# A fused recommendation tower: units of work reordered in phases, preparation on a second DMA queue, gathers paced by products instead of memsets

## What is computed

```python
e = jnp.stack([tbl_f[ids[:, f]] for f in range(39)], axis=1)      # 2048 x 39 x 32
p, q = e[:, ROW, :], e[:, COL, :]                                # the 741 pairs i < j
z = jnp.einsum('bpc,apc,bpa->bp', p, w, q)                       # w: 32 x 741 x 32
h = jnp.concatenate([z, dense_ctx], axis=1)                      # 741 + 16
h = jnp.maximum(h @ W_top1 + b_top1, 0.0)                        # 757 -> 512
h = jnp.maximum(h @ W_top2 + b_top2, 0.0)                        # 512 -> 256
y = h @ W_top3
```

## Time and profile before

| | |
|---|---|
| median of three runs | 873.27 us |
| profiled execution, and its span | 877.21 us, 875.4 us |
| TensorE busy | 734.8 us (84%) |
| VectorE busy | 655.0 us (75%) |
| ScalarE busy | 92.4 us (11%) |
| GpSimd busy: gathers, memsets | 382.3 us, 207.6 us |
| DMA | 149.90 MB, mean 171 GB/s |
| mean granted TensorE clock | 0.93 of 2.4 GHz |

### The profile page before, as it was taken

How to read it: one execution, slowest core, us unless ns; L and a number is a source line. 1 busy time by engine, 2 the same in 40 slices (tenths; PEclk the granted TensorE clock), 3 DMA queues, 4 the chain that set the end, 5 groups by cost and what they waited for, 6 DMA issues and landing times.

```text
span 875.4 us, 11491 instructions
## 1 busy us (share of the span) xinstructions
PE 734.8 (84%) x4378; PEld 291.6 (33%) x4378; DVE 655.0 (75%) x786; ACT 92.4 (11%) x153; POOL 589.1 (67%) x752
## 2 busy tenths in 40 slices
PE   2603567387998969999999699999999799999998
PEld 1201122122332424443433244444433244444333
DVE  4603759466989947899898679999999478998750
ACT  2202000110010101010101111001111010111002
POOL 6899999998169999997599999982999940000000
PEclk9856688788999989999999899999999899999999
DMA  6677663658654567633664647444734575326000
GB/s 162 207 267 271 216 199 106 224 169 288 229 171 159 157 198 227 228 123 101 228 185 154 199 145 244 136 143 164 248 107 154 189 240 172 142 70 207 22 0 1
DMA packets 71036, 149.90 MB, mean 171 GB/s; under 512 B 12782, under 2 KB 22081, under 8 KB 70853
## 3 DMA queue, kind: packets, MB, share of 16 engines
q1 hardware_dynamic: 58684, 142.83, 47.0%
q0 software_dynamic: 12288, 6.32, 5.0%
q10 hardware_dynamic: 8, 0.01, 0.0%
HBM read 115.49 MB, written 33.62 MB: 170 GB/s over the span
## 4 chain that ended last, share of the span: by engine, by line
PE 64%; DMA 14%; DVE 12%; issue 5%; SPq 4%; ACT 1%; DVEq 0%; ACTq 0%
PE z_ps L541 21%; PE u_ps L517 20%; PE t_ps L495 8%; PE m_ps L554 7%; DVE prod L773 6%; DVE one_hot L761 5%; DMA e<-scratch 5%; DMA w_rows<-h 3%; DMA scratch<-parts 3%; PE m_ps L556 2%; DMA hot_idx<-hot 2%; PE t_ps L480 1%; SPq L412 1%; PE u_ps L576 1%; PE u_ps L585 1%
## 5 line engine op out<-in xcount | busy, mean ns | idle before, releaser
L773 DVE TENSOR_TENSOR prod<-u_ps,eT 128x1024 f32<-128x1024 f32 x400 | 469.7, 1216 | 127.6 <-PE u_ps L517 126.6
L330 POOL DMA_INDIRECT e_rows<-in_tbl_dram,idx x384 | 382.3, 996 | 121.4 <-issue 65.3
L517 PE MATMUL u_ps<-e,w 128*128 128x512 f32 x800 | 263.0, 443 | 97.0 <-DMA e<-scratch 50.6
L541 PE MATMUL z_ps<-prod,sel 128*32 128x512 f32 x1600 | 268.7, 624 | 0.0
L517 PEld LDWEIGHTS u_ps<-e,w 128*128 128x128 f32 x800 | 135.6, 195 | 244.2 <-issue 114.4
L337 POOL MEMSET pause<- 128x512 f32 x364 | 207.6, 570 | 0.2
L495 PE MATMUL t_ps<-one_hot,tb 125*32 125x512 bf16 x1560 | 150.2, 399 | 28.2 <-DVE one_hot L761 27.8
L761 DVE TENSOR_SCALAR one_hot<-hot_idx,row 125x512 bf16<-125x512 f16 (+2 forms) x320 | 155.2, 539 | 20.0 <-DMA hot_idx<-hot 16.1
L495 PEld LDWEIGHTS t_ps<-one_hot,tb 125*32 125x32 bf16 x1560 | 56.3, 101 | 124.4 <-issue 82.6
L541 PEld LDWEIGHTS z_ps<-prod,sel 128*32 128x32 f32 x1600 | 44.5, 110 | 141.4 <-issue 122.6
L554 PE MATMUL m_ps<-zT,w1s 128*128 128x512 f32 x144 | 73.2, 592 | 0.0
(11 more groups left out here) (42 smaller groups left out, 101.9 us busy)
## 6 DMA issues: line engine op xcount, KB each, us to landing
w<-w_rows SPq DMA_DIRECT2D x100, 512.0 KB, 5.4
e<-scratch SPq DMA_DIRECT2D x72, 512.0 KB, 4.9
scratch<-parts SPq DMA_DIRECT2D x72, 256.0 KB, 2.2
w_rows<-h SPq DMA_DIRECT2D x24, 512.0 KB, 6.3
e_rows<-in_tbl_dram,idx POOLq DMA_INDIRECT x384
hot_idx<-hot SPq DMA_DIRECT2D x12, 512.0 KB, 6.8
h<-in_w_dram SPq DMA_DIRECT2D x6, 512.0 KB, 4.5
e<-scratch SPq DMA_DIRECT2D x8, 384.0 KB, 4.1
```

Source lines behind the costliest of these rows:

```text
L330: pool.indirect_dma_start(e_rows[:, r, n, D * q:D * q + D], None, tables[f], bass.IndirectOffsetOnAxis(ap=idx[:, t, f * TPG + n:f * TPG + ...
L517: last = nc.tensor.matmul(u_ps[:, s % 2, place, :], w4[:, p % WR, (u % PW) * P:(u % PW + 1) * P], e4[:, chunk_no(t, g) % ES, j - C * g, :] ...
L541: last = nc.tensor.matmul(z_ps[D * quad:D * quad + D, z % 2, :], sel[:, D - 1 - row:2 * D - 1 - row], prod[:, (NS * t + n) % PR, place, :] ...
L773: nc.vector.tensor_tensor(prod[:, s % PR, :, :], u_ps[:, s % 2, :, :], e, ALU.mult).then_inc(s_mul, 1)
```

## The change

**Order of units.** UNITS is built by PHASES = (0, 1, 2, 3, 7, 8, 4, 5, 6, 9): a phase takes the fields of its chunk against all chunks seen so far, and the fields of earlier, higher-numbered chunks against its own. So the looked-up chunks 7 and 8 come before the gathered chunks 4, 5 and 6. Chunks 3, 7, 8, 4, 5, 6 and 9 are first needed as `e4` in batches 5, 9, 13, 21, 28, 36 and 42; chunks 4, 5 and 6 are needed as `eT` two batches before that. The look-ups in FIRST_TILE and OTHER_TILES move with them, mostly two slices per batch, and the pieces of the dense network fill the other batches.

**Slots.** `e4` has four slots, given by chunk (E4_SLOT), so that chunks 0, 1 and 2 of the next tile find theirs free before the tile ends; only chunk 3 waits for chunk 9. The ring of weight pieces shrinks from six to four.

**Preparation.** The weights come in 13 preps of 16 units, in two rooms used in turn. Their DMAs, and those of the tables, are issued by ScalarE. The network's weights are loaded at batch 12 of tile 0.

**Gathers.** Memsets follow gathers only while fewer than 96 were issued. From the 97th gather on (number n counted from 0), GpSimd waits until product n - 39 is done.

```diff
-ES = 3
+ES = 4
+PACED_FROM, PACE_LEAD = 96, 40
+E4_SLOT = {0: 0, 1: 2, 2: 3, 3: 1, 7: 2, 8: 3, 4: 0, 5: 1, 6: 0, 9: 1}
-PREPS = {0: (2,), 3: (3,), 11: (4,), 19: (5,), 27: (6,)}
-PREP_UNITS = [(0, 8)] + [(8 + 32 * k, 40 + 32 * k) for k in range(6)]
+PREP_UNITS = [(16 * k, min(NU, 16 * k + 16)) for k in range(-(-NU // 16))]
+PREPS_FIRST = 3
+PREPS = {4 * (k - PREPS_FIRST): k for k in range(PREPS_FIRST, len(PREP_UNITS))}
-OTHER_TILES = ((3, 0, 0, ()), (4, 0, 3, ()), (5, 0, 7, ()), (6, 0, 12, ()),
-               (7, 0, None, (13, 14, 15, 16, 17, 18, 19, 19, 20, 20)), (8, 0, None, (21, 22, 23, 24, 25, 26, 27, 27, 28, 28)),
+OTHER_TILES = ((3, 0, 0, ()), (7, 0, None, (1, 1, 2, 2, 3, 3, 4, 4, 5, 5)), (8, 0, None, (6, 6, 7, 7, 8, 8, 9, 9, 10, 10)),
+               (4, 0, 14, ()), (5, 0, 20, ()), (6, 0, 27, ()), (9, 0, 35, ()),
...
                     for n in range(TPG):
+                        if issued >= PACED_FROM:
+                            pool.wait_ge(s_mul, issued - PACE_LEAD + 1)
                         pool.indirect_dma_start(
...
-                        if GPOS[c] > 1:
+                        issued += 1
+                        if GPOS[c] > 1 and issued < PACED_FROM:
                             if paused:
                                 pool.wait_ge(s_pause, paused)
                             nc.gpsimd.memset(pause[:, :], 0.0).then_inc(s_pause, 1)
...
+            def weights_rest(k):
+                a, b = PREP_UNITS[k]
+                act.wait_ge(s_wlo, k + 1)
+                for h in range(2):
+                    act.dma_start(w_rows[:, h, 1, a * P:b * P].rearrange("a (s n) -> a s n", s=C),
+                                  w_in_room[k % 2][:, 0:(b - a) * D]).then_inc(s_wout[k % 2], 16)
+                if k + 2 < len(PREP_UNITS):
+                    load_weights(k + 2)
...
+            def load_weights(k):
+                a, b = PREP_UNITS[k]
+                if k >= 2:
+                    act.wait_ge(s_wout[k % 2], 64 * (k // 2))
```

More of the change, by code:

```diff
@@ L23, in fields_in, with hot, gathered @@
     return min(C, F - C * g)
[L27 to L32, removed]
+HOT_TABLES = {1: ((0, 8), (1, 10), (2, 8), (3, 8)), 2: ((1, 8), (2, 8), (3, 8)), 7: ((0, 10), (1, 8), (2, 8), (3, 8)),
+              8: ((0, 10), (1, 8), (2, 10), (3, 10))}
+HOT_CHUNKS = sorted(HOT_TABLES)
+HOT_SLICES = {g: tuple(n for q, n in HOT_TABLES[g]) for g in HOT_CHUNKS}
+def hot(c):
+    return c[1] in HOT_TABLES
+def gathered(c):
+    taken = [q for q, n in HOT_TABLES[c[1]]] if hot(c) else []
+    return [q for q in range(fields_in(c[1])) if q not in taken]
 def slices_of(g):
-    return max(HOT_SLICES[g][1])
+    return max(HOT_SLICES[g])
 def slice_fields(g, k):
-    return [x for x, n in enumerate(HOT_SLICES[g][1]) if n > k]
+    return [x for x, n in enumerate(HOT_SLICES[g]) if n > k]
 HOT_COLS = {}
@@ L132, in rows_count, with e4_before, e4_loads @@
     n = GPOS[c]
-    return sum(16 * TPG * gathered(GATHERED[x][1]) for x in range(n % ER, n + 1, ER))
+    return sum(16 * TPG * len(gathered(GATHERED[x])) for x in range(n % ER, n + 1, ER))
+def e4_before(c):
+    t, g = c
+    same = [x for x in PHASES if E4_SLOT[x] == E4_SLOT[g]]
+    n = same.index(g)
+    return (t, same[n - 1]) if n else (t - 1, same[-1]) if t else None
+def e4_loads(c):
+    same = [x for x in PHASES if E4_SLOT[x] == E4_SLOT[c[1]]]
+    return len(same) * c[0] + same.index(c[1]) + 1
 TURNS, TAKES, COMPLETE, INDICES, STACKS = {}, {}, {}, {}, {}
@@ L166, in spread_mlp @@
         slices = sum(list(x[3]).count(b) for x in OTHER_TILES if not (last and x[1]))
-        work[b] = 3 * slices + (2 if any(x[2] == b for x in OTHER_TILES) else 0)
+        work[b] = 3 * slices + (3 if any(x[2] == b for x in OTHER_TILES) else 0)
     taken = []
@@ L238, in tower @@
         hroom = h1[:, :, :].rearrange("p m n -> p (m n)")
-        w_in_room = hroom[:, 0:2 * NB]
-        w_hi_room = hroom[:, 2 * NB:4 * NB].bitcast(F32R)
+        w_in_room = [hroom[:, k * NB:(k + 1) * NB] for k in range(2)]
+        w_hi_room = [hroom[:, (2 + k) * NB:(3 + k) * NB].bitcast(F32R) for k in range(2)]
         ids_f = prod[:, 0, :, :].rearrange("p u n -> p (u n)")[:, 0:NT * HOT_FIELD_COLS]
         def table_room(g):
-            first, rows = HOT_ROWS[g, 0], sum(HOT_SLICES[g][1])
+            first, rows = HOT_ROWS[g, 0], sum(HOT_SLICES[g])
             if g == HOT_CHUNKS[-1]:
@@ L321, in _ @@
             paused = 0
+            issued = 0
             for c in GATHERED:
@@ L477, in turn @@
                     pe.wait_ge(s_et, POS[c])
-                n = D * gathered(c[1])
+                lo, hi = D * gathered(c)[0], D * (gathered(c)[-1] + 1)
                 for b in range(TPG):
-                    last = nc.tensor.transpose(t_ps[0:n, b * P:b * P + P], e_rows[:, GPOS[c] % ER, b, 0:n], ident[:, :])
+                    rows = e_rows[:, GPOS[c] % ER, b, lo:hi]
+                    if lo == 0:
+                        last = nc.tensor.transpose(t_ps[0:hi, b * P:b * P + P], rows, ident[:, :])
+                    else:
+                        last = nc.tensor.matmul(t_ps[lo:hi, b * P:b * P + P], rows, ident[:, :], start=True, stop=True,
+                                                skip_group_check=True)
                 last.then_inc(s_tp, 1)
@@ L486, in look_up @@
                     pe.wait_ge(s_et, POS[c])
-                if k == 0 and t == 0:
+                if k == 0:
                     pe.wait_ge(s_tlo, HOT_CHUNKS.index(g) + 1)
@@ L595, in _ @@
             transpose_ids()
-            for g, turned, slices in BEGIN:
-                if turned:
+            for g in BEGIN:
+                if gathered((0, g)):
                     turn((0, g))
-                for k in slices:
-                    look_up((0, g), k)
+                if hot((0, g)):
+                    for k in range(slices_of(g)):
+                        look_up((0, g), k)
             pe.wait_ge(s_sel, 16)
```

221 lines of the change are left out of this document (111 added, 110 removed), and 2 rows, old and new, of the table OTHER_TILES.

## The result

The changed kernel takes 842.04 us (841.25 to 842.87, four runs), the kernel before 874.83 in the runs beside it: a ratio of 0.963, with a 95% interval of 0.9605 to 0.965. The forecast was 808, with a range of 784 to 842. The sign was right, but the gain is 33 us and not 67, and the time lies at the range's far end. The profiled execution has a span of 839.4 us, against 875.4.

The account below looks back on a forecast made before the run. No engine full: tile 0 bound by a chain of waits in SyncE's queue, later tiles near TensorE's work, VectorE in some batches. Stalls and clock -27.9, late chunks +4.5, look-ups +5.5, opening and tile 0 -49.3: -67.2, giving 808, range 784 to 842.

Parts of the forecast that it names:

- the walk: Step-by-step timing of opening and tile 0 through the programs; with 6 us added for queueing, tile 1 starts at 251.
- Part 1, the stalls: Batch 2 of tiles 1 to 3: four slots remove waits for chunk 2, 21.9 us, or 27.9 with the clock.
- The slow clock behind the stalls: Tiles 1 to 3: one group of sums takes 3.25 us where 1.07 is usual; 2 each, 6 in all.
- Part 1, late chunks: Tiles 1 to 3: chunk 8, at times 7, a little late; 1.5 us per tile, +4.5, bounds 0 and 5 per tile.
- Part 2 and 3, pairs and memsets: Tiles 1 to 3: paired look-ups lengthen VectorE-bound batches, missing memsets cheapen one-hots; together +1.2, +1.2, +3.1, or +5.5.
- rival B: One-hots: gathers alone hold them up as gathers with memsets did; time 825, chance 0.10.
- Part 4: Opening and tile 0: shorten from 300.3 to 251 us, gain 49.3; ends 232 and 275.
- prep 2's stores land at 58: Opening: stores take 5 us to land (bounds 3.2 and 10.3), at 58; first products at 60 us.
- a count of megabytes up to batch 14: Opening and tile 0: some 30 MB, 120 us at 249 GB/s, under 138, so DMA bandwidth isn't the bound, though near.
- A: Tile 0: ScalarE becomes the gate, nine preps cost 3 us more each; time 835, chance 0.17.
- C: Turns behind tile 0: paced gathers come late, slower than before; 892 at 4 late, 934 at 6; chance 0.05.
- D: Opening and tile 0: the timing is too careful, tile 0 ends at 232; time 789, chance 0.10.

Follow-up runs that it names:

- experiment 8: Kernel before with only the look-ups of the next tile's chunks 1 and 2 moved earlier, chunk 2's done in batch 47 instead of 49: 851.92 us, ratio 0.974.
- (9): Kernel before with both four slots given by chunk and the earlier look-ups of experiment 8: 849.72 us, ratio 0.972.
- (7): Kernel before with four slots given by chunk and four rooms for weight pieces, look-ups and memsets as before: 871.68 us, ratio 0.996.
- Experiment 2: Changed kernel with the look-ups of chunk 8 in tiles 1 to 3 dealt one batch earlier: 830.8 us, ratio 0.951 to the kernel before.
- (3): Changed kernel with the edits of gate and Experiment 2 together: 819.72 us, ratio 0.940 to the kernel before.
- three_first: Kernel of (3) with chunk 3 turned in batch 0 of tile 0, ahead of chunk 7's look-ups: 807.93 us, ratio 0.925 to the kernel before.
- (4): Changed kernel with memsets between the gathers kept throughout and no pacing by products: 871.2 us, ratio 0.998 to the kernel before.
- gate: Changed kernel with ScalarE issuing raw weights of preps 4 and 5 after tile 0's casts, not behind landings of preps 2 and 3: 829.93 us, ratio 0.950.
- Experiment 12: The run of three_first: kernel of (3) with chunk 3 turned in batch 0 of tile 0, ahead of chunk 7's look-ups: 807.93 us, ratio 0.925.
- (5): Changed kernel without the wait that paces gathers by products, still no memsets from the 96th gather on: 840.35 us, ratio 0.962 to the kernel before.
- early_nomem: Kernel of (9) with no memsets from the 96th gather on: 842.41 us, ratio 0.964 to the kernel before.

## Why the prediction was half right

Two terms of the sum failed. Opening and tile 0 were to give 49.3 us and gave 26.4: the walk had the stores of prep 2 landing at 58, and they landed at 73, with ScalarE and behind it the first products waiting. Late chunks were charged 4.5 us in tiles 1 to 3 and cost 9 to 12.

**Part 1, the stalls: near in size, wrong in cause.** They are gone. The forecast was 27.9 us; the table alone gives 22.6 (experiment 8) and with the slots 24.8 (9). But the prediction says that the slot "frees only when the tile before ends", and that four slots take this away. Four slots alone do not (7). The stack stood behind look-ups that ended in batch 49. That the change also ended them in batch 47 I had counted only under the pairs. I read the last condition off the program and did not look which of the two came last; the queue's rows would have told. The slow clock behind the stalls was priced at 2 us each, by a group of sums of another batch (1.07). The same group takes 1.91 without a stall (8), against 3.25, 2.90 and 2.83 with one, so the price is 3.3 us in all and not 6.

**Part 1, late chunks: a term that was mis-sized.** I charged 1.5 us per tile for chunk 8, with 5 as the bound if two chunks were late. The pause is 2.2 to 2.5 us, and the four pieces behind it take 1.3 to 1.5 more. Experiment 2 gives 11 us back (9 in the profiled executions), and with the opening mended too (3) the three tiles are 3.4, 3.3 and 4.9 us shorter, 11.7 in all. I had priced the slow clock behind the old stalls and not behind the new one.

**Part 2 and 3, pairs and memsets: right for the changed kernel, with the memsets priced too low.** Before, without stall and slow clock (by the 1.91), tiles 1, 2 and 3 take 176.5, 175.9 and 197.5 us. In `three_first`, where chunk 8 is in time, they take 176.8, 176.7 and 200.2: +0.3, +0.8 and +2.7, where the sum said +1.2, +1.2 and +3.1. The one-hot at 351 ns makes rival B wrong. What I had as the price of the memsets, 6.3 us a tile (7.5 less 1.2), is too low: putting them back costs 12.0, 9.1 and 8.9 (4). Beside memsets the wide forms in pairs take 806 ns and not 694, which is a part of it; the rest I can't name.

**Part 4: the steps of the walk.** The walk's marks beside the traces (us; "batch 5" is where it goes on behind its wait):

| | walk | changed | `gate` | `three_first` |
|---|---|---|---|---|
| first product | 60 | 75.1 | 63.5 | 63.2 |
| products of batch 1 | 73 | 87.3 | 76.3 | 76.7 |
| turn of chunk 3 | 81 | 100.2 | 87.6 | 66.0 |
| batch 5 | 99 | 119.5 | 107.6 | 93.8 |
| batch 9 | 120 | 138.2 | 127.2 | 116.0 |
| batch 14 | 138 | 162.6 | 151.7 | 140.4 |
| tile 1 | 251 | 273.9 | 263.2 | 252.2 |

Look-ups began at 20.3 us (forecast 19.4), table 7 was split at 32.0 (31). The step that failed is "prep 2's stores land at 58": 15 us. Chunk 2 was taken at 55.14 and not 49, and one issue took 4.24 us and not 0.6, so the last store went out at 61.37 and not 53, and it landed after 11.76 us and not 5. Around it the DMA engines moved 323 GB/s (55 to 75 us), more than the 249 that I read over a longer stretch. The sum there, a count of megabytes up to batch 14, hid that peak, though the trace of before has one like it:

```profile
75.00:95.00 20.00, 8.24 (x28) 2.94 (x28) 6.09 (x7) 2.12 (x3) 18.01 (x26) 0.67 0.84 304
```

That the traffic made the landing long is argued from the two standing side by side. What is shown is that ScalarE's wait for it costs 12 us (1).

Batch 5 came 20.5 us late: 15 from the start, 4 more in the batches before the turn of chunk 3, and only 1.3 on chunk 3's own way back, 19.3 us from turn to resumption where the walk has 18. The second step that failed is chunk 8 in tile 0: from batch 9 to batch 14 the walk has 18 us and the trace 24.3, with a wait of 6.4 us for chunk 8. No run took that wait away.

Experiment 12 must not be read as mending the walk. The wait on chunk 3 was in the forecast (products of batch 4 at 87, batch 5 at 99); turning chunk 3 first removes a stall that the walk had counted in. With only the failed step mended, in `gate`, tile 1 starts at 263.2. That `three_first` has it at 252.2, beside my 251, is a coincidence of one saving that I had not planned and the losses that remained.

**Rivals.** A named the right engine and the wrong place: ScalarE's waits for landings cost in the opening, not in batches 14 to 36, where VectorE waits 1.3 us in all for the rounding between 162 and 230 us. C did not come: no turn waits on `e_rows`, and the pacing is idle (5). D did not come.

**The sum.** Forecast 67: opening 49, tiles 18. Measured 36 in the profiled executions: 26 and 10. The tiles' part divides into stalls and clock -25.2, pairs without memsets +3.8, and late chunks +11.9 (changed kernel less `three_first`), where the forecast had -27.9, +5.5 and +4.5. The parts by experiment: the table with early look-ups 22.6, slots about 2, memsets in the old order 7.3 on top (849.72 to 842.41), and phases, pairs and opening together nothing, as +18 in the opening and -20 in the tiles. This division holds for this order of the edits; in the changed kernel the missing memsets alone are worth 29 (4). Nor do phases and pairs gain in tiles 1 to 3 once chunk 8 is in time: `three_first` beats `early_nomem` by 34 us, with 40 won up to tile 1 and 2 to 3 lost in every tile behind it. What stays open is how much of the opening's 18 us is the second queue and how much the order of units. A kernel with the old order in tiles 1 to 3 and the new opening was not tried.

## What to carry to other kernels

Where two conditions hold a transfer, undo each alone before you credit either: the large edit here (slots) was worth 2 to 4 us, and a row of a table 22. A stall that an edit creates also costs the work behind it at the lower clock (here 1.5 us behind a stall of 2.2), so price both, and take the normal length from the same instructions in a run without the stall. A wait for a landing on an engine that also feeds others should be priced by the window of 20 us around it, not by the mean of the stage; if it isn't needed then, move it.

## What was not expected of the hardware

- Beside gathers that each have a memset of 128x512 behind them, the 512 one-hot takes 524 ns, 49% more than the 351 beside gathers alone; gathers alone cost next to nothing (351 paced and 357 unpaced, 346 with GpSimd idle). The same memsets cost 11 us in one order of the look-ups and 29 in the other.
- One DMA issue can hold the issuing engine for 4.24 us (median 0.62 over the span) while the engines move 323 GB/s. The same issue takes 3.67 us in `gate` and 3.10 in `three_first`.
- Behind an idle stretch of TensorE of 2.20 us the granted clock was 0.55 for 3.4 us, and four matmuls took 3.39 us instead of 1.88.
